# Three chunk copies of an attention kernel moved from ACT to DVE, and its square roots moved up

## The chip, the cores and the metric

The kernel runs on one core of a Trainium2 chip. A core has five engines that run side by side and meet through semaphores: PE (matrix products), DVE (vector work), ACT (activations), POOL (a second, more general vector engine) and SP, which here only issues transfers. The metric is device time in microseconds (us), lower is better.

## The reference

The inputs are x and a context, 16 batches of 64 channels by 512 columns each, in single precision. Per batch:

```python
qp = Wq @ instance_norm(layernorm(x)) + bq;  kp = Wk @ instance_norm(ctx) + bk;  sp = Ws @ ctx + bs
attn = softmax(qp.T @ kp)                      # 512 x 512
mean, mean_sq = attn weighted sums of sp and sp * sp
std = sqrt(relu(mean_sq - mean * mean))
x = x + tanh(g_xattn) * (instance_norm(ctx) * std + mean)
x = x + tanh(g_ffn) * (layernorm(x) @ w.T)     # w dequantised, 512 x 512
```

## The kernel before

Two batches are stacked on the 128 partitions, so there are 8 tiles of 128 x 512 (`t`, or `u` behind attention). Attention works on chunks of 128 columns of one batch: 4 per batch, 8 per tile, 64 in all; `g` is the chunk's number over all tiles, `c` its number in the tile. Every engine has a program of its own in a fixed order written out by hand, and each engine carries out its list strictly in that order; only semaphores tie them together.

One chunk passes through: scores on PE (L292, L293), the row maximum on DVE (L619), the exponential on ACT (L442), the reciprocal of the row sum on DVE (L626), normalising on POOL (L834), the turn on PE (`turn`, four transposes into one of two banks of PSUM, `turn_bank`, L302), the copy of the turned chunk from PSUM to SBUF on ACT (`keep_turned`, L450, into one of three buffers `probs_t`) and the weighted sums on PE (`weigh`, L318). PE turns chunk g, then weighs chunk g-2. A turn needs its bank free, so turn(g) waits for the copy of chunk g-2, and weigh(g) waits for the copy of chunk g.

When a batch's four chunks are weighed, ACT copies the mean (`keep_mean`, L457) and squares it (L460), and DVE subtracts it to the variance (`variance`, L637). Per tile POOL then clips the variance (`relu`, L844), ACT takes its square root (`root`, L465), the normalised context is multiplied with the root, for tile 0 on DVE (`scale_first_context`, L664) and for tiles 1 to 7 on POOL (`scale_context`, L863), and DVE adds the product to X (`after_attention`, L670). The mean was added to X before (`with_mean`, L631).

The last stage, the feed-forward, takes X tile by tile: PE turns it (`turn_x`, L353), ACT copies the turned tile (`keep_xt_hi`, L477), DVE takes the remainder (`keep_xt_lo`, L687), and PE multiplies (L367, L368 with the copy, L374 with the remainder). Beside it DVE takes the row statistics (`row_statistics`, L676, and `finish_row_statistics`, L680 and L682), POOL makes a scale from them (`inverse_deviation2`, L868 and L872), and DVE adds the result to X (`add_ffn`, L695), which SP stores.

The square root needs another function table than the exponential, and is put behind the last exponential for that. In the lists of the engines around the end of attention stand, before the change:

- ACT: exponential of chunk 63, copy of chunk 60, root(0), copies of chunks 61 and 62, keep_mean(7, 0), root(1), copy of chunk 63, keep_xt_hi(0), root(2), root(3), keep_mean(7, 1), keep_xt_hi(1), root(4), keep_xt_hi(2), and so on.
- DVE: reciprocal of chunk 63, with_mean(6), scale_first_context, after_attention(0), variance(7, 0), row_statistics(0), after_attention(1), finish_row_statistics(0), keep_xt_lo(0), row_statistics(1), after_attention(2), finish_row_statistics(1), keep_xt_lo(1), row_statistics(2), variance(7, 1), add_ffn(0), finish_row_statistics(2), after_attention(3), and so on.
- POOL: normalising of chunk 63, the last remainder of the weights (`weights_lo(3)`, L855), scale_context(1), scale_context(2), inverse_deviation2(0), scale_context(3), inverse_deviation2(1), relu(7), scale_context(4), inverse_deviation2(2), scale_context(5), and so on. scale_context(u) waits for root(u), scale_context(1) for scale_first_context too, relu(7) for variance(7, 1).
- PE: turn(62), weigh(60), turn(63), weigh(61), turn_x(0), weigh(62), weigh(63), turn_x(1), the products of tile 0 with the copy, turn_x(2), those with the remainder, and so on.

The functions and the lists that the change touches:

Of the kernel before, what the change touches and what calls it, by code (L numbers as in the profile page):

```python
# [18 lines left out]
def gated_attention_ffn(nc, x, context, params, weight_q_t, scales_zeros, out):  # L19
# [5 lines left out]
    AHEAD_S, AHEAD_E, BEHIND_V = 3, 2, 2  # L25
    SBANKS, PROBS, PROBS_T = 3, 4, 3
    LAST = CHUNKS * TILES
    DMA = 16
    STACK = 6 * DMA
    assert 2 * C == P and N == 512 and GROUPS == 4 and TILES == 8  # L30
# [5 lines left out]
    with ExitStack() as ctx:  # L36
# [9 lines left out]
        def sem(name):  # L46
            return ctx.enter_context(nc.semaphore(name))
# [36 lines left out]
        probs_t = [sb(f"probs_t{i}", [P, N]) for i in range(PROBS_T)]  # L84
# [24 lines left out]
        turn_bank = [bank(f"turn_bank{i}") for i in range(2)]  # L109
# [47 lines left out]
        probs_done = sem("probs_done")  # L157
        turned = sem("turned")
        turned_kept = sem("turned_kept")
        pv_done = sem("pv_done")  # L160
        mean_kept = sem("mean_kept")
        mean_squared = sem("mean_squared")
# [108 lines left out]
        def _(pe):  # L271
# [11 lines left out]
            def scores(g):  # L283
# [5 lines left out]
                if g >= SBANKS:  # L289
# [3 lines left out]
                pe.matmul(score_bank[g % SBANKS][:, :], q_part, k_cross[b][:, :],  # L293
                          start=False, stop=True).then_inc(scores_done, 1)

            def turn(g):

                pe.wait_ge(probs_done, g + 1)
                if g >= 2:
                    pe.wait_ge(turned_kept, g - 1)  # L300
                for i in range(JC):
                    last = pe.transpose(turn_bank[g % 2][:, P * i:P * i + P],  # L302
                                        probs[g % PROBS][:, P * i:P * i + P], ident[:, :])
                last.then_inc(turned, 1)

            def weigh(g):

                t, c = divmod(g, CHUNKS)
                b, j = divmod(c, JC)
                pe.wait_ge(turned_kept, g + 1)  # L310
                if j == 0:
                    pe.wait_ge(s_squared, t + 1)
                    if t > 0:
                        pe.wait_ge(var_done, 2 * (t - 1) + b + 1)
                    elif b == 0:
                        pe.wait_ge(k_lo_done, 1)
                for i in range(JC):
                    last = pe.matmul(pv_bank[b][:, P * j:P * j + P],  # L318
                                     values[t % 2][:, i, b, :, :].rearrange("p a c -> p (a c)"),
                                     probs_t[g % PROBS_T][:, P * i:P * i + P], start=(i == 0), stop=(i == JC - 1))  # L320
                last.then_inc(pv_done, 1)
# [66 lines left out]
            for t in range(TILES):  # L388
                for c in range(CHUNKS):
                    g = CHUNKS * t + c  # L390
# [33 lines left out]
        @block.scalar  # L424
        def _(act):
            def keep_hi(t, which):

                hi, used, done = ((q_hi, q_done, q_hi_done), (k_hi, k_done, k_hi_done))[which]
                act.wait_ge(used, t + 1)
                if t >= 2:  # L430
                    act.wait_ge(stacked[0], STACK * (t - 1))
                    act.wait_ge(stacked[1], STACK * (t - 1))
                act.activation(hi[t % 2][:, :], projection_bank(t, which)[:, :], ACT.Identity,  # L433
                               bias=b_qk[:, which:which + 1]).then_inc(done, 1)

            def exponentials(g):

                c = g % CHUNKS
                act.wait_ge(max_done, g + 1)
                if g >= PROBS:  # L440
                    act.wait_ge(turned, g - PROBS + 1)
                act.activation(probs[g % PROBS][:, :], score_bank[g % SBANKS][:, :], ACT.Exp,  # L442
                               bias=neg_max[:, c:c + 1], accum_out=den[:, c:c + 1]).then_inc(exp_done, 1)

            def keep_turned(g):

                act.wait_ge(turned, g + 1)
                if g >= PROBS_T:
                    act.wait_ge(pv_done, g - PROBS_T + 1)
                act.copy(probs_t[g % PROBS_T][:, :], turn_bank[g % 2][:, :]).then_inc(turned_kept, 1)  # L450

            def keep_mean(t, b):

                act.wait_ge(pv_done, CHUNKS * t + JC * b + JC)
                if t >= 2:
                    act.wait_ge(mean_added, t - 1)
                act.copy(MEAN[t % 2][rows_of(b), :], pv_bank[b][0:C, :]).then_inc(mean_kept, 1)  # L457
                if t >= 1:
                    act.wait_ge(var_done, 2 * (t - 1) + b + 1)
                act.activation(mean_sq[b][C:P, :], pv_bank[b][0:C, :], ACT.Square).then_inc(mean_squared, 1)  # L460

            def root(u):

                act.wait_ge(relu_done, u + 1)
                act.activation(VAR[:, u, :], VAR[:, u, :], ACT.Sqrt).then_inc(root_done, 1)  # L465

            def weights_hi(g):

                act.wait_ge(w_centred, g + 1)
                act.copy(w_hi[:, g, :], w_deq[:, g, :]).then_inc(ffn_hi_done, 1)  # L470

            def keep_xt_hi(u):

                act.wait_ge(xt_turned, u + 1)
                if u >= 2:
                    act.wait_ge(ffn_done, u - 1)
                act.copy(xt_hi[u % 2][:, :], xt_bank[u % 2][:, :]).then_inc(xt_hi_done, 1)  # L477


            act.wait_ge(params_loaded, DMA)  # L480
            act.copy(w_qk_hi[:, :, :], w_qk).then_inc(w_hi_ready, 1)
            act.activation(tanh_g[:, :], gates, ACT.Tanh).then_inc(gates_ready, 1)
            for part, whole, whole_done, part_done in ((x_hi, xn[:, :], xn_done, x_hi_done),
                                                       (c_hi, CTX[:, 0, :], ctxn_done, c_hi_done)):
                act.wait_ge(whole_done, 1)
                act.copy(part[:, :], whole).then_inc(part_done, 1)
            keep_hi(0, 0)
            keep_hi(0, 1)
            act.wait_ge(k_hi_done, 1)
            act.copy(k_same[0][0:C, :], k_hi[0][0:C, :].bitcast(F32)).then_inc(stacked[0], DMA)  # L490
            act.copy(k_cross[0][C:P, :], k_hi[0][0:C, :].bitcast(F32)).then_inc(stacked[0], DMA)
            for g in range(AHEAD_E):
                exponentials(g)

            for t in range(TILES):
                for c in range(CHUNKS):
                    g = CHUNKS * t + c
                    if g + AHEAD_E < LAST:
                        exponentials(g + AHEAD_E)
                    elif c == 6:  # L500
                        root(0)
                    if g > 0:
                        keep_turned(g - 1)
                    if t == 0 and c < 2:
                        keep_hi(1, c)
                    if c == 0 and t > 0 and t + 1 < TILES:
                        keep_hi(t + 1, 1)
                    if c == 2 and t > 0:
                        keep_mean(t - 1, 1)
                    if c == 6 and t + 2 < TILES:  # L510
                        keep_hi(t + 2, 0)
                    if c == 7:
                        keep_mean(t, 0)
                    if t == TILES - 1 and 1 <= c <= 4:
                        weights_hi(c - 1)

            root(1)
            keep_turned(LAST - 1)
            keep_xt_hi(0)
            root(2)  # L520
            root(3)
            keep_mean(TILES - 1, 1)
            keep_xt_hi(1)
            root(4)
            keep_xt_hi(2)
            root(5)
            keep_xt_hi(3)
            root(6)
            keep_xt_hi(4)
            root(7)  # L530
            for u in range(5, TILES):
                keep_xt_hi(u)
# [3 lines left out]
        def _(dve):  # L536
# [85 lines left out]
            def reciprocal(g):  # L622

                c = g % CHUNKS
                dve.wait_ge(exp_done, g + 1)
                dve.reciprocal(rden[:, c:c + 1], den[:, c:c + 1]).then_inc(rden_done, 1)  # L626

            def with_mean(t):

# [4 lines left out]
            def variance(t, b):  # L634

                dve.wait_ge(mean_squared, 2 * t + b + 1)
                dve.tensor_tensor(VAR[rows_of(b), t, :], pv_bank[b][C:P, :], mean_sq[b][C:P, :],  # L637
                                  ALU.subtract).then_inc(var_done, 1)
# [89 lines left out]
            for t in range(TILES):  # L728
                for c in range(CHUNKS):
                    g = CHUNKS * t + c  # L730
# [41 lines left out]
                    if t == TILES - 1:  # L772
                        if c < GROUPS:
                            centre_weights(c)
                        if c == 7:
                            scale_first_context()
                            after_attention(0)

            variance(TILES - 1, 0)
            row_statistics(0)  # L780
            after_attention(1)
# [184 lines left out]
```

## Time and profile before

| | us |
|---|---|
| median of 3 runs | 189.22 |
| the runs | 189.13, 189.22, 190.19 |
| the profiled execution's own time | 190.1 |
| span of its trace | 188.3 |

| engine | busy in the span, us | share |
|---|---|---|
| PE | 169.9 | 90% |
| DVE | 147.1 | 78% |
| ACT | 123.1 | 65% |
| POOL | 118.2 | 63% |

The granted clock of PE is at its full level in all forty slices of the span. All times of rows are us from the start of the span. A row of a timeline has the start, the duration, the engine, the line, the operation, what it writes and reads, and in brackets how long the engine sat idle before it and what ended that. An operation's recorded duration can reach a little over the start of the next one on the same engine.

### The profile page before, as it was taken

The page shows a single profiled execution, that of the slowest core. Times are in us where ns is not written, and L with a number is a line of the kernel's source. Part 1 is how long each engine was busy: PE and PEld are TensorE (multiplying, and loading weights), DVE is VectorE, ACT ScalarE, POOL GpSimd, SP SyncE. Part 2 cuts the span into 40 slices and gives each one's busy share as a digit, 9 for nine tenths or more (in the row PEclk, how much of TensorE's full clock was granted, in tenths as well). Part 3 has the DMA queues.
Part 4 walks back from the last instruction along what each step waited for, and adds up shares of the span by engine and source line. Part 5 has one row for each costly group of instructions (what it writes and reads, how often), then busy time and mean ns, then how long its engine had stood idle before and what let it go on. Part 6 is the DMA issues. An engine that isn't in the chain of part 4 may idle for free.

```text
span 188.3 us, 3539 instructions
## 1 busy us (share of the span) xinstructions
PE 169.9 (90%) x1144; PEld 147.8 (78%) x1144; DVE 147.1 (78%) x316; ACT 123.1 (65%) x268; POOL 118.2 (63%) x142
## 2 busy tenths in 40 slices
PE   0249799999999999999999999999999979789993
PEld 0228599999999989998998999898789778567781
DVE  2888869788978998798889879766248778988851
ACT  2356565996789588669957866995569997223110
POOL 1216667736947795699569669934526969966410
PEclk9999999999999999999999999999999999999999
DMA  5249545761895687289549728353300000111212
GB/s 181 91 121 225 155 111 131 227 148 34 197 308 140 139 286 216 54 205 328 123 108 282 223 59 183 94 118 77 91 0 3 0 0 0 56 57 59 111 56 111
DMA packets 13281, 24.05 MB, mean 128 GB/s; under 512 B 2128, under 2 KB 2256, under 8 KB 13264
## 3 DMA queue, kind: packets, MB, share of 16 engines
q1 hardware_dynamic: 13264, 23.83, 45.8%
q8 instruction: 9, 0.15, 0.3%
q14 instruction: 8, 0.07, 0.1%
HBM read 9.67 MB, written 2.10 MB: 62 GB/s over the span
## 4 chain that ended last, share of the span: by engine, by line
PE 76%; DVE 10%; ACT 5%; issue 3%; DMA 2%; POOL 2%; SPq 0%; ACTq 0%; DVEq 0%
PE pv_bank L318 26%; PE turn_bank L302 13%; PE score_bank L292 8%; PE score_bank L293 8%; PE side_bank L330 3%; PE score_bank L374 3%; PE score_bank L368 2%; PE score_bank L367 2%; PE side_bank L279 2%; DMA params_sb<-in_params 2%; DVE X L670 2%; PE side_bank L281 2%; PE side_bank L280 2%; PE side_bank L339 2%; ACT probs_t L450 1%
## 5 line engine op out<-in xcount | busy, mean ns | idle before, releaser
L834 POOL TENSOR_SCALAR probs<-probs,rden 128x512 f32<-128x512 f32 x64 | 51.3, 803 | 36.1 <-DVE rden L626 35.9
L318 PE MATMUL pv_bank<-probs_t,values 128*128 128x128 f32 x512 | 67.4, 275 | 0.0
L318 PEld LDWEIGHTS pv_bank<-probs_t,values 128*128 128x128 f32 x512 | 63.3, 192 | 2.5 <-issue 1.4
L619 DVE TENSOR_REDUCE neg_max<-score_bank 128x1 f32<-128x512 f32 x64 | 44.0, 687 | 23.6 <-PE score_bank L293 23.2
L442 ACT ACTIVATE probs<-score_bank,neg_max 128x512 f32<-128x512 f32 x64 | 44.0, 688 | 25.0 <-DVE neg_max L619 24.6
L302 PEld LDWEIGHTS turn_bank<-ident,probs 128*128 128x128 f32 x256 | 31.5, 141 | 11.5 <-POOL probs L834 2.4
L302 PE MATMUL turn_bank<-ident,probs 128*128 128x128 f32 x256 | 38.5, 273 | 2.1 <-ACT probs_t L450 1.2
L450 ACT COPY probs_t<-turn_bank 128x512 f32<-128x512 f32 x64 | 37.0, 580 | 0.0
L292 PE MATMUL score_bank<-k_same,q_stack 128*128 128x512 f32 x64 | 31.1, 487 | 2.5 <-DVE k_cross L717 2.5
L293 PE MATMUL score_bank<-k_cross,q_stack 128*128 128x512 f32 x64 | 26.0, 407 | 0.0
L292 PEld LDWEIGHTS score_bank<-k_same,q_stack 128*128 128x128 f32 x64 | 12.7, 198 | 3.5 <-DVE k_cross L717 3.3
L293 PEld LDWEIGHTS score_bank<-k_cross,q_stack 128*128 128x128 f32 x64 | 12.7, 198 | 0.2
L367 PE MATMUL score_bank<-w_hi,xt_hi 128*128 128x512 f32 x32 | 12.8, 401 | 0.0
L368 PE MATMUL score_bank<-w_lo,xt_hi 128*128 128x512 f32 x32 | 12.7, 396 | 0.0
L442 ACT ACTIVATION_READ_ACCUMULATOR probs<-score_bank,neg_max 128x1 f32 x64 | 12.5, 195 | 0.0
L821 POOL TENSOR_TENSOR x_lo<-xn,x_hi 128x512 fp32r<-128x512 f32 x7 | 8.9, 1275 | 5.3 <-DVE x_hi L593 5.3
L279 PE MATMUL side_bank<-x_hi,w_qk_hi 128*128 128x512 f32 x8 | 4.3, 533 | 8.1 <-DVE x_lo L706 8.1
L637 DVE TENSOR_TENSOR VAR<-pv_bank,mean_sq 64x512 f32<-64x512 f32 x16 | 11.1, 694 | 0.5
L626 DVE RECIPROCAL rden<-den 128x1 f32<-128x1 f32 x64 | 9.8, 153 | 1.7 <-ACT probs L442 1.5
L868 POOL TENSOR_TENSOR rstd<-var_eps,power 128x1 f32<-128x1 f32 x8 | 6.7, 834 | 7.0 <-DVE var_eps L682 7.0
L863 POOL TENSOR_TENSOR CTX<-CTX,VAR 128x512 f32<-128x512 f32 x7 | 9.4, 1346 | 2.1 <-ACT VAR L465 2.1
L433 ACT ACTIVATE q_hi<-side_bank,params_sb 128x512 fp32r<-128x512 f32 x8 | 5.5, 687 | 7.5 <-PE side_bank L281 7.5
(101 smaller groups left out, 270.7 us busy)
## 6 DMA issues: line engine op xcount, KB each, us to landing
X<-in_x SPq DMA_DIRECT2D x8, 256.0 KB, 3.1
CTX<-in_context SPq DMA_DIRECT2D x8, 256.0 KB, 3.9
q_stack<-q_hi SPq DMA_DIRECT2D x16, 128.0 KB, 2.3
q_stack<-q_lo SPq DMA_DIRECT2D x16, 128.0 KB, 2.4
ctx_now<-in_context SPq DMA_DIRECT2D x8, 256.0 KB, 3.0
sz<-in_scales_zeros SPq DMA_DIRECT2D x4, 512.0 KB, 6.2
out<-result SPq DMA_DIRECT2D x8, 256.0 KB, 2.0
k_same<-k_hi SPq DMA_DIRECT2D x15, 128.0 KB, 2.4
```

What stands on the lines that cost most here:

```text
L292: pe.matmul(score_bank[g % SBANKS][:, :], q_part, k_same[b][:, :], start=True, stop=False)
L293: pe.matmul(score_bank[g % SBANKS][:, :], q_part, k_cross[b][:, :], start=False, stop=True).then_inc(scores_done, 1)
L302: last = pe.transpose(turn_bank[g % 2][:, P * i:P * i + P], probs[g % PROBS][:, P * i:P * i + P], ident[:, :])
L318: last = pe.matmul(pv_bank[b][:, P * j:P * j + P], values[t % 2][:, i, b, :, :].rearrange("p a c -> p (a c)"), probs_t[g % PROBS_T][:, P * ...
L367: pe.matmul(ffn_bank[u % 2][:, :], hi, w_hi[:, g, :], start=(g == 0), stop=False)
L368: pe.matmul(ffn_bank[u % 2][:, :], hi, w_lo[:, g, :], start=False, stop=False)
L442: act.activation(probs[g % PROBS][:, :], score_bank[g % SBANKS][:, :], ACT.Exp, bias=neg_max[:, c:c + 1], accum_out=den[:, c:c + 1]).then_ ...
L450: act.copy(probs_t[g % PROBS_T][:, :], turn_bank[g % 2][:, :]).then_inc(turned_kept, 1)
L619: dve.tensor_reduce(neg_max[:, c:c + 1], score_bank[g % SBANKS][:, :], AX_X, ALU.max, negate=True).then_inc(max_done, 1)
L626: dve.reciprocal(rden[:, c:c + 1], den[:, c:c + 1]).then_inc(rden_done, 1)
L637: dve.tensor_tensor(VAR[rows_of(b), t, :], pv_bank[b][C:P, :], mean_sq[b][C:P, :], ALU.subtract).then_inc(var_done, 1)
L834: pool.tensor_scalar(probs[g % PROBS][:, :], probs[g % PROBS][:, :], rden[:, c:c + 1], 1.0, ALU.mult, ALU.mult).then_inc(probs_done, 1)
```

## The change

The copies of chunks 61, 62 and 63 are made by DVE (`keep_last_turned`) and counted on a semaphore of their own; PE waits for the one or the other by the chunk's number (`wait_turned_kept`). On ACT they are left out, and root(2) moves ahead of keep_xt_hi(0). ACT's list becomes: copy of chunk 60, root(0), keep_mean(7, 0), root(1), root(2), keep_xt_hi(0), root(3), keep_mean(7, 1), keep_xt_hi(1), and on as before. DVE's becomes: with_mean(6), copies of chunks 61 and 62, scale_first_context, after_attention(0), copy of chunk 63, variance(7, 0), row_statistics(0), after_attention(1), and on as before. POOL's and PE's lists keep their order.

```diff
+    LAST_TURNED = 3
...
+            def wait_turned_kept(g):
+
+                if g < LAST - LAST_TURNED:
+                    pe.wait_ge(turned_kept, g + 1)
+                else:
+                    pe.wait_ge(last_turned_kept, g - (LAST - LAST_TURNED) + 1)
+
             def turn(g):
 
                 pe.wait_ge(probs_done, g + 1)
                 if g >= 2:
-                    pe.wait_ge(turned_kept, g - 1)
+                    wait_turned_kept(g - 2)
...
-                pe.wait_ge(turned_kept, g + 1)
+                wait_turned_kept(g)
...
-                    if g > 0:
+                    if 0 < g <= LAST - LAST_TURNED:
                         keep_turned(g - 1)
...
             root(1)
-            keep_turned(LAST - 1)
+            root(2)
             keep_xt_hi(0)
-            root(2)
             root(3)
...
+            def keep_last_turned(g):
+
+                dve.wait_ge(turned, g + 1)
+                dve.wait_ge(pv_done, g - PROBS_T + 1)
+                dve.tensor_copy(probs_t[g % PROBS_T][:, :], turn_bank[g % 2][:, :]).then_inc(last_turned_kept, 1)
...
-                        if c == 7:
+                        if c == 6:
+                            keep_last_turned(LAST - 3)
+                            keep_last_turned(LAST - 2)
                             scale_first_context()
                             after_attention(0)
 
+            keep_last_turned(LAST - 1)
             variance(TILES - 1, 0)
             row_statistics(0)
             after_attention(1)
```

## Rows read from the trace of the kernel before

**Rows 1.** The chain that ended last: start, us, what; from 140 us on.
```profile
154.62 1.28 POOL CTX L863
...
167.78 0.65 PE side_bank L353 x4
...
185.04 0.75 DVE result L695
```

**Rows 2.** Timeline of ACT from the table of the square root on.
```profile
149.92 1.28 ACT L465 ACT_TABLE_LOAD   x1
151.21 0.63 ACT L465 ACTIVATE VAR<-VAR 128x512 f32<-128x512 f32 x1
151.75 1.05 ACT L450 COPY probs_t<-turn_bank 128x512 f32<-128x512 f32 x2
152.69 0.58 ACT L457 COPY MEAN<-pv_bank 64x512 f32<-64x512 f32 x1
...
153.91 0.63 ACT L465 ACTIVATE VAR<-VAR 128x512 f32<-128x512 f32 x1
```

**Rows 3.** Timeline of PE, the turn of chunk 63.
```profile
152.46 0.63 PE L302 MATMUL turn_bank<-ident,probs 128*128 128x128 f32 x4 [0.90 <-ACT probs_t L450]
```

**Rows 4.** Timeline of DVE.
```profile
149.54 1.41 DVE L631 SCALAR_TENSOR_TENSOR X<-MEAN,tanh_g,X 128x512 f32<-128x512 f32 x1
151.88 1.42 DVE L664 TENSOR_TENSOR CTX<-CTX,VAR 128x512 f32<-128x512 f32 x1 [0.93 <-ACT VAR L465]
153.33 0.75 DVE L670 SCALAR_TENSOR_TENSOR X<-CTX,tanh_g,X 128x512 f32<-128x512 f32 x1
154.11 0.69 DVE L637 TENSOR_TENSOR VAR<-pv_bank,mean_sq 64x512 f32<-64x512 f32 x1
154.83 0.69 DVE L676 BATCH_NORM_STATS2 stats<-X 128x6 f32<-128x512 f32 x1
155.93 0.75 DVE L670 SCALAR_TENSOR_TENSOR X<-CTX,tanh_g,X 128x512 f32<-128x512 f32 x1 [0.40 <-POOL CTX L863]
...
156.81 0.15 DVE L682 TENSOR_SCALAR var_eps<-mean_var 128x1 f32<-128x1 f32 x1
156.99 0.69 DVE L687 TENSOR_TENSOR xt_lo<-side_bank,xt_hi 128x512 fp32r<-128x512 f32 x1
157.60 0.68 DVE L676 BATCH_NORM_STATS2 stats<-X 128x6 f32<-128x512 f32 x1
158.20 0.73 DVE L670 SCALAR_TENSOR_TENSOR X<-CTX,tanh_g,X 128x512 f32<-128x512 f32 x1
...
162.12 1.52 DVE L670 SCALAR_TENSOR_TENSOR X<-CTX,tanh_g,X 128x512 f32<-128x512 f32 x1
...
179.86 0.15 DVE L682 TENSOR_SCALAR var_eps<-mean_var 128x1 f32<-128x1 f32 x1
```

**Rows 5.** Timeline of POOL.
```profile
151.48 1.26 POOL L855 TENSOR_TENSOR w_lo<-w_deq,w_hi 128x512 fp32r<-128x512 f32 x1
...
156.11 1.71 POOL L863 TENSOR_TENSOR CTX<-CTX,VAR 128x512 f32<-128x512 f32 x1 [0.21 <-ACT VAR L465]
...
158.94 1.28 POOL L863 TENSOR_TENSOR CTX<-CTX,VAR 128x512 f32<-128x512 f32 x1
...
161.81 1.28 POOL L863 TENSOR_TENSOR CTX<-CTX,VAR 128x512 f32<-128x512 f32 x1
...
168.21 0.19 POOL L872 TENSOR_TENSOR scale<-rstd,tanh_g 128x1 f32<-128x1 f32 x1
168.35 1.29 POOL L863 TENSOR_TENSOR CTX<-CTX,VAR 128x512 f32<-128x512 f32 x1
...
180.09 0.55 POOL L868 TENSOR_TENSOR rstd<-var_eps,power 128x1 f32<-128x1 f32 x1 [1.53 <-DVE var_eps L682]
```

**Rows 6.** Costliest groups of the page: operation, count, busy, mean ns, idle before.
```profile
L619 DVE TENSOR_REDUCE neg_max<-score_bank 128x1 f32<-128x512 f32 x64 | 44.0, 687 | 23.6 <-PE score_bank L293 23.2
```

**Rows 7.** One line's instructions: DVE's copy L605, ns minimum, median, maximum.
```profile
L605 DVE CAST c_hi<-CTX x7: 585/587/1051, 17.8 to 117.3; 128x512 fp32r<-128x512 f32 x7
```

More of the change, by code:

```diff
@@ L159, in gated_attention_ffn @@
         turned_kept = sem("turned_kept")
+        last_turned_kept = sem("last_turned_kept")
         pv_done = sem("pv_done")
```

## The prediction, made before the change was run

> **What bounds the kernel now.** I read the page's busy shares first, then the chain that ended last, then the timelines of the four engines from 149 us on, where the first changed instruction stands. PE is busy 90% of the span, but that is a mean over stages. From 167.78 us on the chain lies on PE, up to the last result at 185.04 [rows 1]. Before that it does not: it comes from ACT's roots over POOL's multiplication of tile 1's context [rows 1] to DVE, whose list then runs with no gap to speak of until PE takes over. So the change is worth what it does to the moment at which DVE gets through its list between 150 and 168 us. Work taken from ACT or PE in that stretch counts only if DVE gets something earlier from it.
>
> Two stalls of DVE are plain idle time there: 0.93 us for root(0) ahead of L664, and 0.40 for POOL ahead of after_attention(1) [rows 4]. A third kind is hidden in durations. L664 took 1.42 us beside a POOL operation that ended at 151.48 + 1.26 = 152.74, and itself ended at 153.30; after_attention(3) took 1.52 beside one that ended at 161.81 + 1.28 = 163.09, and ended at 163.64 [rows 4, 5]. The same operation takes 0.75 without company. So a DVE operation with two operands in SBUF that meets a running POOL operation ends 0.55 us behind POOL's end, and it works the other way too: scale_context(2) took 1.71 in place of 1.28 beside after_attention(1), ending 1.71 - 1.28 = 0.43 late, as if begun at 156.54, 0.14 before DVE's end at 156.68 [rows 4, 5]. Whichever starts first keeps the other out. An operation with one operand in SBUF is not held: L676 at 154.83 takes its 0.69 beside scale_context(1), which runs from 154.62 to 155.90 [rows 1, 4].
>
> **The change part by part.** *PE.* turn(63) sat idle 0.90 us for ACT's copy of chunk 61, which stood behind the table load and root(0) [rows 2, 3]. That copy now starts on DVE behind with_mean(6), at 149.54 + 1.41 = 150.95 [rows 4], in place of 151.75. So turn(63) and weigh(61) come some 0.8 us earlier. Nothing follows from it: PE's next instruction is turn_x(0), which waits for after_attention(0), and weigh(62) and weigh(63) stand behind that in PE's list. This gain is worth 0.
>
> *The copies' price.* No DVE copy from PSUM is in the trace. The nearest rows are the maximum, which reads the same shape from PSUM in 0.69 [rows 6], and the copy from SBUF, 0.59 alone and 1.05 when held [rows 7]. I take 0.69, with 0.59 and 1.05 as ends. Their own gain of 0.1 each is too small to matter below; being held would matter and is a rival.
>
> The Trainium skill speaks of this in "VectorE: DVE Perf Modes", section "Why PSUM operands drop a tier": a PSUM operand rules out the mode that uses both SBUF ports, so by that page the copy from PSUM would neither run at the doubled rate nor be held by POOL. By that rule the sum is the one below and the third rival falls; by the row of the SBUF copy alone the rival stands. No run here shows the copy itself.
>
> *Copies 61 and 62.* 150.95 + 2 x 0.69 = 152.33. Then comes L664, which root(0) releases at 151.84 as before; it meets the POOL operation that runs until 152.74 and ends at 153.30 as before. The two copies are hidden by the 0.93 idle and 0.45 of the hold; without that cover they would cost 1.38. after_attention(0) is unchanged, 153.33 to 154.08.
>
> *The roots.* root(0) stays at 151.21. Without the two copies the mean's copy starts at 151.75 in place of 152.69, so root(1), 153.91 - 152.69 = 1.22 behind it, starts at 152.97 and ends at 153.61, 0.94 earlier [rows 2]; root(2) follows at once and ends by 153.61 + 0.63 = 154.24. scale_context(1), released by root(1) at about 153.68, finds after_attention(0) running since 153.33 and begins in effect at 154.08 - 0.14 = 153.94; it ends at 153.94 + 1.28 = 155.22, not 154.62 + 1.28 = 155.90. scale_context(2) has its root by then and follows with no gap, 155.2 to 156.48. Before, it came only at 156.11, behind after_attention(1), for want of root(2) [rows 5].
>
> *Copy 63.* It stands on DVE between after_attention(0) and variance(7, 0): 154.08 + 0.69 = 154.77, variance from 154.80, statistics 0.72 later (154.83 - 154.11) at 155.52, after_attention(1) due 0.6 to 0.7 behind, 156.0 to 156.2. This one is not hidden: the 0.40 idle covers part, and after_attention(1) is due 0.1 to 0.3 later than its 155.93 of before.
>
> *What is late next.* At 156.1 POOL is inside scale_context(2). So after_attention(1) is held and ends at 156.48 + 0.55 = 157.03, where it was 155.93 + 0.75 = 156.68: +0.35. This hardly depends on the copy's price, since POOL's end sets it. Then DVE's list runs on as before, 0.35 later: L682 at 156.81 + 0.35 = 157.16, after_attention(2) due at 158.55. POOL is idle now, where before it was still late from its own hold. It takes L868 0.23 behind L682 (180.09 - 179.86), which lasts 0.55, L872 0.08 behind that (the step from L682's end at 180.01 to L868), and scale_context(3) 0.14 behind L872's start [rows 4, 5]: 157.16 + 0.23 + 0.55 + 0.08 + 0.14 = 158.16, until 159.44. Before, scale_context(3) started at 158.94, behind after_attention(2); now it starts 0.39 ahead of it. after_attention(2) is held and ends at 159.44 + 0.55 = 159.99, where it was 158.20 + 0.73 = 158.93: +1.06.
>
> From there POOL's relu(7) waits for DVE's variance(7, 1), so scale_context(4) and the hold of after_attention(3) come again at the same distance. The +1.06 passes on whole to PE at 167.78, which had waited for DVE, and to the end. ACT's and PE's waits in that stretch all hang on DVE's after_attention or on PE's products, which have over half a microsecond to spare.
>
> The sum: PE 0, copies 61 and 62 0, copy 63 and the first collision +0.35, the second +0.71; together +1.06. Against the profiled execution that is 190.1 + 1.06 = 191.16 (span 188.3 to 189.36). The runs' median, 189.22, lies 0.9 below that execution, so the forecast for a median is 189.22 + 1.06 = 190.28, say 190.3.
>
> **The rivals.** *Only the first collision.* If DVE reaches after_attention(2) before POOL starts scale_context(3), the price stays at +0.35: 189.6. The margin is 0.39, and some 0.3 if L687 follows L682 sooner than the 0.18 of before. For it: the margin is a difference of two sums of several steps each, POOL's taken from other tiles. Against: all steps but the first are DVE's and POOL's own work with nothing to wait for.
>
> *DVE goes first (not slower).* If after_attention(1) starts ahead of scale_context(2), both collisions fall, POOL is again the one held, and DVE's list runs as before. The point of decision is whether scale_context(2) starts before 156.0 to 156.2. Priced at 0.59 a copy from 153.99 on, as the pipeline allows where nothing is held, after_attention(1) is due at 155.9 and the 0.40 idle is just used up: 0.0 to -0.2, 189.0 to 189.2. For it: so it was before [rows 4, 5]. Against: scale_context(2) would have to come 0.8 later than its root allows.
>
> *The copies are held too (slower by over 1%).* If a copy from PSUM needs the port like L605's slow case, copy 62 waits for POOL until 152.74 and ends near 153.3, so L664 ends at 154.0 and after_attention(0) at 154.8, +0.7; copy 63 is then held by scale_context(1), 1.3 more, and the second collision stays at +0.7: +2.7 in all, 191.9. The point of decision is the duration of copy 62: 0.69 or over 1. Against: none of the PSUM readers is stretched.
>
> *It doesn't do what it says.* If something else held root(1), say keep_mean's wait for weigh(59), POOL would start no earlier and only copy 63's 0.1 to 0.3 would be left: 189.4. But weigh(59) stands two places ahead of turn(63) in PE's list, with weigh(60) between them, and PE had been idle since 151.56 when turn(63) began [rows 3], so weigh(59) was done well before 151.56.
>
> **How the numbers follow.** The forecast 0.62; only the first collision 0.14; DVE first 0.09; copies held 0.07; no earlier root 0.04; something that the rows don't show 0.04, half to each side. What a measurement can tell from no change is about 1%, 1.9 us: below 187.3 or above 191.1. The forecast and all rivals but the held copies lie inside. Slower by over 1%: 0.07 and some of the unknown, 0.10. Faster: all idle time of DVE in the stretch together is 1.33 us, less than 1.9, so 0.03. Within: 0.87. The range goes from 189.0 (DVE first) to 191.1 (the forecast with another half hold of 0.8); it leaves out the held copies, half of the unknown cases and the lower part of "DVE first".
>
> **What would show it right or wrong.** In the changed profile: copies on DVE of about 0.69 at 150.9, 151.6 and 154.0; turn(63) near 151.6; L664 again ending at 153.3; root(1) at 153.0; scale_context(1) stretched beyond 1.28 and scale_context(2) right behind it; after_attention(1) and after_attention(2) both stretched to over 0.9 us, where they were 0.75 and 0.73; turn_x(4) on PE 1.06 later, and the same distance to the end. I am wrong if the two after_attention rows stay at 0.75 (the collisions don't come), if copy 62 is over 1 us, or if turn_x(4) comes before 167.78.

## The result, and the profile after

The changed kernel takes 190.32 us (median of 12 runs, 189.62 to 191.25), the kernel before 189.34 beside it (12 runs, 188.94 to 190.19). The ratio is 1.0054, 95% interval 1.0030 to 1.0078: 0.6 to 1.5 us slower, some 1.0. The profiled execution took 191.25 with a span of 189.5, against 190.1 and 188.3.

Up to the last exponential the two programs are the same, and there the changed one is 0.09 us late (its start is at 148.71, before at 148.62). What follows is best read from that point on. The row of the kernel before from which its times are counted:

```profile
148.62 0.71 ACT L442 ACTIVATE probs<-score_bank,neg_max 128x512 f32<-128x512 f32 x1
```

ACT's timeline of the changed kernel, which answers to [rows 2]:

```profile
148.71 0.71 ACT L451 ACTIVATE probs<-score_bank,neg_max 128x512 f32<-128x512 f32 x1
...
150.00 1.28 ACT L474 ACT_TABLE_LOAD   x1
151.29 0.63 ACT L474 ACTIVATE VAR<-VAR 128x512 f32<-128x512 f32 x1
151.83 0.56 ACT L466 COPY MEAN<-pv_bank 64x512 f32<-64x512 f32 x1
...
153.03 1.15 ACT L474 ACTIVATE VAR<-VAR 128x512 f32<-128x512 f32 x2
```

root(1) starts at 153.03 where it was 153.91, and root(2) is in the same row, right behind it. That part of the change does what it says. PE's turn of chunk 63, which answers to [rows 3], has lost its wait:

```profile
151.79 0.63 PE L311 MATMUL turn_bank<-ident,probs 128*128 128x128 f32 x4
...
154.23 0.66 PE L362 MATMUL side_bank<-ident,X 128*128 128x128 f32 x4 [0.92 <-DVE X L684]
```

It starts at 151.79, not 152.46, and has no idle in front of it. The next row shows what that is worth: turn_x(0) starts at 154.23, 0.09 later than the 154.14 of before, after 0.92 us of waiting for DVE, where it was 0.15. The stall has only moved. DVE's timeline, which answers to [rows 4]:

```profile
149.62 1.43 DVE L645 SCALAR_TENSOR_TENSOR X<-MEAN,tanh_g,X 128x512 f32<-128x512 f32 x1
150.97 1.27 DVE L640 COPY probs_t<-turn_bank 128x512 f32<-128x512 f32 x2
152.17 1.22 DVE L678 TENSOR_TENSOR CTX<-CTX,VAR 128x512 f32<-128x512 f32 x1
153.43 0.75 DVE L684 SCALAR_TENSOR_TENSOR X<-CTX,tanh_g,X 128x512 f32<-128x512 f32 x1
154.09 0.68 DVE L640 COPY probs_t<-turn_bank 128x512 f32<-128x512 f32 x1
154.81 0.69 DVE L651 TENSOR_TENSOR VAR<-pv_bank,mean_sq 64x512 f32<-64x512 f32 x1
155.53 0.69 DVE L690 BATCH_NORM_STATS2 stats<-X 128x6 f32<-128x512 f32 x1
156.14 0.95 DVE L684 SCALAR_TENSOR_TENSOR X<-CTX,tanh_g,X 128x512 f32<-128x512 f32 x1
...
158.62 1.47 DVE L684 SCALAR_TENSOR_TENSOR X<-CTX,tanh_g,X 128x512 f32<-128x512 f32 x1
...
163.28 1.52 DVE L684 SCALAR_TENSOR_TENSOR X<-CTX,tanh_g,X 128x512 f32<-128x512 f32 x1
```

Look at the L684 rows, the additions after attention: 0.75 for tile 0, then 0.95 and 1.47 for tiles 1 and 2, which were 0.75 and 0.73, and 1.52 for tile 3 as before. POOL's timeline, which answers to [rows 5], shows with whom they meet:

```profile
151.57 1.27 POOL L872 TENSOR_TENSOR w_lo<-w_deq,w_hi 128x512 fp32r<-128x512 f32 x1
153.74 2.81 POOL L880 TENSOR_TENSOR CTX<-CTX,VAR 128x512 f32<-128x512 f32 x2 [0.89 <-ACT VAR L474]
157.45 0.56 POOL L885 TENSOR_TENSOR rstd<-var_eps,power 128x1 f32<-128x1 f32 x1 [0.91 <-DVE var_eps L696]
158.09 0.19 POOL L889 TENSOR_TENSOR scale<-rstd,tanh_g 128x1 f32<-128x1 f32 x1
158.24 1.30 POOL L880 TENSOR_TENSOR CTX<-CTX,VAR 128x512 f32<-128x512 f32 x1
...
164.21 1.00 POOL L885 TENSOR_TENSOR rstd<-var_eps,power 128x1 f32<-128x1 f32 x1
```

scale_context(1) and (2) are now one block, until 153.74 + 2.81 = 156.55, and after_attention(1), due at 156.14, ends at 157.09, 0.54 behind the block. scale_context(3) starts at 158.24, 0.38 ahead of after_attention(2), and ends at 159.54; after_attention(2) ends at 160.09, 0.55 behind it. Before it ended at 158.93, so it is 1.16 late, 1.07 without the 0.09 that came from ahead of the change. turn_x(4), with which the chain goes over to PE, starts at 168.94 where it was 167.78 [rows 1]: again 1.16. Its row, and that of the last result:

```profile
168.94 0.66 PE L362 MATMUL side_bank<-ident,X 128*128 128x128 f32 x4 [0.62 <-DVE X L684]
```
```profile
186.21 0.75 DVE L709 SCALAR_TENSOR_TENSOR result<-score_bank,scale,X 128x512 f32<-128x512 f32 x1 [2.06 <-PE score_bank L383]
```

The start of the last result lies 37.50 us behind the start of the last exponential; before it was 36.42. The difference, 1.08, is the whole loss.

### The profile page after: what moved, and what is told of

The parts are those of the page before. It is cut to its first block, busy times and chain, and to the rows that moved or that the text cites. A ratio compares the mean times of both kernels' runs of the same rounds, so it can differ in the third digit from the quotient of the medians.

```text
span 189.5 us, 3539 instructions
## 1 busy us (share of the span) xinstructions
PE 170.4 (90%) x1144; PEld 148.0 (78%) x1144; DVE 149.5 (79%) x319; ACT 121.3 (64%) x265; POOL 117.2 (62%) x142
## 4 chain that ended last, share of the span: by engine, by line
PE 74%; DVE 13%; issue 4%; ACT 3%; DMA 2%; POOL 2%; SPq 0%; ACTq 0%; DVEq 0%
PE pv_bank L327 25%; PE turn_bank L311 13%; PE score_bank L295 7%; PE score_bank L294 7%; PE side_bank L339 3%; PE score_bank L383 3%; PE side_bank L281 3%; PE score_bank L377 2%; PE score_bank L376 2%; DVE X L684 2%; DMA params_sb<-in_params 2%; PE side_bank L283 2%; PE side_bank L282 2%; PE side_bank L348 2%; DVE stats L690 1%
## 5 line engine op out<-in xcount | busy, mean ns | idle before, releaser
L311 PEld LDWEIGHTS turn_bank<-ident,probs 128*128 128x128 f32 x256 | 32.1, 143 | 10.5 <-issue 1.4
L311 PE MATMUL turn_bank<-ident,probs 128*128 128x128 f32 x256 | 39.1, 276 | 0.9 <-POOL probs L851 0.5
L459 ACT COPY probs_t<-turn_bank 128x512 f32<-128x512 f32 x61 | 35.3, 579 | 0.0
L885 POOL TENSOR_TENSOR rstd<-var_eps,power 128x1 f32<-128x1 f32 x8 | 6.7, 835 | 8.8 <-DVE var_eps L696 8.8
L856 POOL TENSOR_TENSOR values<-values 128x512 f32<-128x512 f32 x8 | 9.1, 1139 | 2.8 <-DVE values L660 2.8
L442 ACT ACTIVATE q_hi<-side_bank,params_sb 128x512 fp32r<-128x512 f32 x8 | 5.5, 687 | 7.5 <-PE side_bank L283 7.4
```

Source lines behind the costliest of these rows:

```text
L311: last = pe.transpose(turn_bank[g % 2][:, P * i:P * i + P], probs[g % PROBS][:, P * i:P * i + P], ident[:, :])
```

## The experiments

All the versions below share the program up to the last exponential, but their executions reach it between 147.4 and 149.5 us. So beside each measured ratio stands the distance in its profile from the start of the last exponential (L442 in the kernel before) to the start of the last result (L695), which that scatter does not touch. For the kernel before it is 36.42. Each distance comes from one profile, but the parts of it that no version changes repeat closely: from the last exponential to turn_x(0) it is 5.52 or 5.53 in all eleven profiles, and from turn_x(7) to the last result 6.25 or 6.26. PE's granted clock is at its full level (2.4 GHz) from the last exponential to the end in all of them.

The kernel before ran again beside the versions of each round: its median was 189.84 beside e1 to e4, 189.77 beside e5 to e7 and 189.92 beside e8 and e9. The ratios go by these runs, not by the 189.34 above, and they are not the quotients of the medians (for e1 that would be 189.46 / 189.84 = 0.998).

| version | ratio to before, 95% interval | distance, us | against before |
|---|---|---|---|
| changed kernel | 1.0054 (1.0030 to 1.0078) | 37.50 | +1.08 |
| e1, POOL waits twice | 0.9994 (0.9971 to 1.0018) | 36.52 | +0.10 |
| e3, POOL waits once | 1.0005 (0.9974 to 1.0035) | 36.77 | +0.35 |
| e2, copy 63 on ACT | 1.0051 (1.0024 to 1.0078) | 37.48 | +1.06 |
| e4, before with root(2) up | 1.0089 (1.0057 to 1.0121) | 38.15 | +1.73 |
| e5, copy 63 on ACT and both waits | 0.9960 (0.9930 to 0.9991) | 35.94 | -0.48 |
| e6, before with two meetings less | 0.9966 (0.9935 to 0.9998) | 36.00 | -0.42 |
| e7, e5 and e6 together | 0.9932 (0.9908 to 0.9957) | 35.15 | -1.27 |
| e8, e7 with the mean later | 0.9895 (0.9860 to 0.9929) | 34.48 | -1.94 |
| e9, e6 with the mean later | 0.9918 (0.9883 to 0.9953) | 35.34 | -1.08 |

Two explanations of the loss were to be told apart: that POOL's multiplications, coming earlier, keep DVE's additions out (called the port theory below), or that DVE simply has three copies more to do (work). The profile alone can't decide this, since both make DVE late.

**Take the meetings away, keep the work (e1).** POOL waits for DVE's addition before its next multiplication:

```diff
             def scale_context(u):
 
                 pool.wait_ge(root_done, u + 1)
                 if u == 1:
                     pool.wait_ge(scaled_done, 1)
+                if u in (2, 3):
+                    pool.wait_ge(x2_done, u)
```

> The changed kernel, with POOL's scale_context(2) and scale_context(3) waiting until DVE has done after_attention(1) and after_attention(2). Port theory: both after_attention rows are back at 0.75 us, only the place of copy 63 in DVE's list is left of the price: +0.2 us against the kernel before (189.3 to 189.7). Rival, that DVE's three added copies (about 1.9 us of work) are the price and the stretched rows only show them: the waits can only delay POOL, so the time stays at the changed kernel's 190.3 or is longer.

Measured: 189.46 us (median of 12), ratio 0.9994 against the kernel before, no difference to be seen, and 0.10 us more by the profile. The same three copies are on DVE, and adding two waits to POOL took the loss away. DVE's and POOL's timelines show the rows back at their price:

```profile
156.31 0.73 DVE L684 SCALAR_TENSOR_TENSOR X<-CTX,tanh_g,X 128x512 f32<-128x512 f32 x1
...
158.56 0.73 DVE L684 SCALAR_TENSOR_TENSOR X<-CTX,tanh_g,X 128x512 f32<-128x512 f32 x1
```
```profile
157.19 1.29 POOL L882 TENSOR_TENSOR CTX<-CTX,VAR 128x512 f32<-128x512 f32 x1 [1.71 <-DVE X L684]
...
159.44 1.29 POOL L882 TENSOR_TENSOR CTX<-CTX,VAR 128x512 f32<-128x512 f32 x1
```

POOL now sits idle for 1.71 us ahead of scale_context(2), and the kernel is 0.98 us faster by the profile than the changed one for it.

**Take only the second away (e3).** The same edit with `if u in (3,)`.

> The changed kernel, with scale_context(3) alone waiting for after_attention(2). Port theory: after_attention(1) stays stretched at 0.95, after_attention(2) is back at 0.75; +0.35 us against the kernel before (189.5 to 189.9), so 0.7 less than the changed kernel. Rival (work): as the changed kernel, 190.3.

Measured: 189.73 us, ratio 1.0005; by the profile +0.35. DVE's two rows are as expected, the first held and the second not:

```profile
155.88 0.95 DVE L684 SCALAR_TENSOR_TENSOR X<-CTX,tanh_g,X 128x512 f32<-128x512 f32 x1
...
158.35 0.74 DVE L684 SCALAR_TENSOR_TENSOR X<-CTX,tanh_g,X 128x512 f32<-128x512 f32 x1
```

So the first meeting with copy 63 in DVE's list is worth 0.35, and the second the other 0.73.

**Take work away, keep the meetings (e2).** Copy 63 goes back to ACT, behind the two early roots:

```diff
             root(1)
             root(2)
+            keep_turned(LAST - 1)
             keep_xt_hi(0)
...
-            keep_last_turned(LAST - 1)
             variance(TILES - 1, 0)
```

PE's `wait_turned_kept` is told accordingly that chunk 63 counts on ACT's semaphore again.

> The changed kernel with the copy of chunk 63 back on ACT, behind root(2); copies 61 and 62 stay on DVE, the roots stay early. Port theory: DVE reaches after_attention(1) 0.7 us earlier but finds scale_context(2) at work since 155.2 and ends when it did: the row is stretched to 1.4 or more, the rest as in the changed kernel, +1.0 us against the kernel before (190.1 to 190.6). Rival (work): DVE has 0.7 us less to do, so +0.35 (189.7).

Measured: 190.80 us, ratio 1.0051, and by the profile +1.06, as if nothing had been taken from DVE. The row of after_attention(1) has taken up what the copy left:

```profile
155.38 1.55 DVE L686 SCALAR_TENSOR_TENSOR X<-CTX,tanh_g,X 128x512 f32<-128x512 f32 x1
...
158.45 1.47 DVE L686 SCALAR_TENSOR_TENSOR X<-CTX,tanh_g,X 128x512 f32<-128x512 f32 x1
```
```profile
153.58 2.80 POOL L881 TENSOR_TENSOR CTX<-CTX,VAR 128x512 f32<-128x512 f32 x2 [0.91 <-ACT VAR L475]
```

It starts earlier and ends at 156.93, 0.55 behind POOL's block of two, 153.58 + 2.80 = 156.38. The work theory wanted 0.7 us less and falls here.

**Make the meetings without any copy (e4).** In the kernel before, root(2) moves up by two places on ACT, and nothing else:

```diff
             root(1)
+            root(2)
             keep_turned(LAST - 1)
             keep_xt_hi(0)
-            root(2)
             root(3)
```

> The kernel before with root(2) moved up behind root(1), ahead of the copy of chunk 63 and keep_xt_hi(0); no copy on DVE. Port theory: scale_context(2) now follows scale_context(1) with no gap, at 155.86, a hair ahead of after_attention(1), which ends at 157.69 (+1.0); scale_context(3) then starts at 158.8, ahead of after_attention(2) due at 159.2, which ends at 160.65: +1.7 us against the kernel before (190.7 to 191.3), with no work added anywhere. If DVE wins the near tie at 155.9: 0. Rival (work): no change, 189.3.

Measured: 191.10 us, ratio 1.0089, by the profile +1.73: 1.6 times the loss of the whole change, from one instruction that became ready earlier. DVE's rows, and POOL's block of scale_context(1) and (2):

```profile
154.83 1.75 DVE L670 SCALAR_TENSOR_TENSOR X<-CTX,tanh_g,X 128x512 f32<-128x512 f32 x1 [0.39 <-POOL CTX L863]
...
158.10 1.47 DVE L670 SCALAR_TENSOR_TENSOR X<-CTX,tanh_g,X 128x512 f32<-128x512 f32 x1
```
```profile
153.53 2.50 POOL L863 TENSOR_TENSOR CTX<-CTX,VAR 128x512 f32<-128x512 f32 x2 [1.87 <-ACT VAR L465]
```

The 0.39 of waiting for scale_context(1) is still there, and behind it the same operation that took 0.75 takes 1.75, because scale_context(2) started at the moment at which scale_context(1) let DVE go. The near tie at 155.9 went to POOL.

**Keep what is good in the change (e5).** e2 with the two waits of e1.

> Copies 61 and 62 on DVE, copy 63 on ACT, early roots, and scale_context(2) and (3) waiting for after_attention(1) and (2). Port theory: after_attention(1) starts as soon as scale_context(1) lets it, some 0.4 us earlier than in the kernel before, both rows at 0.75: -0.4 us against the kernel before (ratio 0.998), 1.4 less than without the waits. Rival (work): the waits change nothing, as in the run without them (ratio 1.005).

Measured: 189.05 us against 189.77, ratio 0.9960; by the profile -0.48. The first addition that gains is after_attention(1):

```profile
155.04 0.73 DVE L686 SCALAR_TENSOR_TENSOR X<-CTX,tanh_g,X 128x512 f32<-128x512 f32 x1
```

It starts 6.83 us behind the last exponential (at 148.21 in this profile), where it was 7.31: this is the 0.48. scale_context(1), for which it had waited, ends at 6.60 instead of 7.27, since root(1) comes earlier with copies 61 and 62 gone from ACT. So the change holds a gain, once POOL doesn't get in front of DVE with it. Whether root(2)'s move adds to it behind the two waits was not tried.

**Take away meetings that were there before (e6).** In the kernel before:

```diff
             scale_context(3)
+            scale_context(4)
             inverse_deviation2(1)
             relu(TILES - 1)
-            scale_context(4)
...
             row_statistics(3)
-            with_mean(TILES - 1)
             add_ffn(1)
...
                 if u + 1 < TILES:
                     row_statistics(u + 1)
+                if u == 4:
+                    with_mean(TILES - 1)
                 add_ffn(u - 1)
```

> The kernel before with two later collisions taken out and no copy moved: POOL's scale_context(4) ahead of inverse_deviation2(1) and relu(7), so that it is done when DVE reaches after_attention(3), and DVE's with_mean(7) moved behind row_statistics(5), where PE is the bound. Port theory: after_attention(3) falls from 1.52 to 0.75 us and the 1.34 of with_mean(7) leaves DVE's full stretch; PE's idle 1.18 and 0.62 us ahead of turn_x(3) and turn_x(4) shrink to some 0.4: -1.0 to -1.5 us (ratio 0.992 to 0.995). If DVE were not the bound there: no change.

Measured: ratio 0.9966, by the profile -0.42. The size was missed by more than half. turn_x(4) did come 1.12 earlier from the last exponential (18.04 us behind it, not 19.16), and after_attention(3) takes 0.75. But with_mean(7) met scale_context(7) at its new place, and PE paid for it:

```profile
169.91 1.35 DVE L631 SCALAR_TENSOR_TENSOR X<-MEAN,tanh_g,X 128x512 f32<-128x512 f32 x1
```
```profile
169.42 1.30 POOL L864 TENSOR_TENSOR CTX<-CTX,VAR 128x512 f32<-128x512 f32 x1
```
```profile
172.93 0.66 PE L353 MATMUL side_bank<-ident,X 128*128 128x128 f32 x4 [0.62 <-DVE X L670]
```

The rows are DVE's with_mean(7), POOL's scale_context(7) and PE's turn_x(6). I had priced the move at 0.75 and not asked who runs beside the new place.

**Both together (e7).**

> The two before together: copies 61 and 62 on DVE, copy 63 on ACT, early roots, the two waits on POOL, scale_context(4) earlier and with_mean(7) later. Port theory: the gains add until PE has no idle left in the stretch, 1.18 + 0.62 us: -1.4 to -1.8 us against the kernel before (ratio 0.990 to 0.993), faster than both kernels.

Measured: 188.41 us against 189.77, ratio 0.9932; by the profile -1.27, short of the -1.4 to -1.8 by the same meeting, which is there too (with_mean(7) takes 1.35, and PE sits idle 0.63 us ahead of turn_x(6)). It is still more than e5 and e6 give one by one, 0.48 + 0.42 = 0.90: in e6 DVE sits idle 0.28 us ahead of after_attention(4), for which the profile names no releaser, and in e7 it doesn't. Why was not tried.

**The mean one tile later (e8 and e9)**, `if u == 5`, where POOL has no context left. e8 is e7 with this, e9 is e6 with it:

> The version with all edits, with_mean(7) one tile later, behind row_statistics(6). In the version before, it stood beside scale_context(7), took 1.35 us and made PE idle 0.63 ahead of turn_x(6). One tile later POOL has no context left to multiply and turn_x(7) comes only behind the products with the remainder. Port theory: with_mean(7) at 0.75, no idle of PE ahead of turn_x(6) and turn_x(7): 0.6 us less than before, ratio 0.989 to 0.992. If the order alone counts and not the meeting: as before, 0.993.

> The kernel before with scale_context(4) earlier and with_mean(7) behind row_statistics(6), no copy moved, no root moved. Port theory: as the version with it one tile earlier but 0.6 us less: ratio 0.992 to 0.995; it stays some 0.4 us behind the version with all edits, by the earlier after_attention(1).

Measured: 188.05 us against 189.92, ratio 0.9895 for e8 (6 runs), and 0.9918 (188.27, 7 runs) for e9, at the lower edge of its 0.992 to 0.995. In e8's profile with_mean(7) is unheld and turn_x(6) has no idle:

```profile
173.91 0.73 DVE L647 SCALAR_TENSOR_TENSOR X<-MEAN,tanh_g,X 128x512 f32<-128x512 f32 x1
```
```profile
172.85 0.66 PE L363 MATMUL side_bank<-ident,X 128*128 128x128 f32 x4
```

By the profiles the step from u = 4 to u = 5 is worth 0.67 (35.15 to 34.48) and 0.66 (36.00 to 35.34). e8 is 0.86 ahead of e9 by the profiles, more than the 0.4 expected; the medians' ratios, 0.9895 and 0.9918, put it at 0.44 with intervals that overlap, so how much the copies and the early roots bring on top of the rest is not settled. e8 is the fastest of all versions, by some 2.0 us ahead of the kernel before and, by way of it, 3.0 ahead of the changed one, beside which it did not run (1.0054 - 0.9895 = 0.016 of 189).

## Why the prediction was right

Forecast 190.3, measured 190.32. A median that close has luck in it, since the runs scatter by over 1 us; the steps are what can be judged, and they can be judged one by one. The profiles put the loss at 1.08 where 1.06 was forecast; the medians of 12 runs each differ by 190.32 - 189.34 = 0.98. The prediction took about 1% for what a measurement can tell; with these runs the interval of the ratio reaches 0.24% to either side, enough to tell 0.54% from nothing.

- *PE's earlier turn is worth 0.* Right: turn(63) came 0.67 earlier (0.76 without the 0.09 from ahead of the change) and turn_x(0) 0.09 later, with 0.92 of idle ahead of it in place of 0.15.
- *The copies at 0.69, unheld.* Right: 0.68, and 1.27 for two, while POOL was at work beside both. The rival of held copies falls. The rule of the Trainium skill that the prediction set beside it ("VectorE: DVE Perf Modes", "Why PSUM operands drop a tier") agrees with the trace: the copies took 0.68, neither the 0.43 of the cast from SBUF that ran with POOL idle (L593, below) nor a stretched time.
- *Copies 61 and 62 hidden.* Right: L678 ended at 153.39, before at 153.30, and the 0.09 was there already at the last exponential. Its duration fell from 1.42 to 1.22, because it started later, behind the copies, and POOL's operation ended as before.
- *root(1) at 152.97, scale_context(1) held by after_attention(0), scale_context(2) with no gap, ending at 156.48.* Right: 153.03, and 156.55 for the block; without the 0.09, 152.94 and 156.46. e4, with root(1) where it was and no copy on DVE, shows separately that root(2) alone can bring the meetings about.
- *First meeting +0.35, whatever the copy costs.* Right: 157.09 - 156.68 - 0.09 = 0.32 in the changed kernel, 0.35 in e3. That POOL's end sets it, and not the copy, is e2's finding.
- *Second meeting, decided by a margin of 0.39.* Right: 0.38. The rival with only the first meeting fell with it, as e3 gives its time, +0.35.
- *The rest passes on whole.* Right: +1.07 at after_attention(2), 1.07 at turn_x(4), 1.08 at the last result.
- *DVE goes first* was the way to end level; e1 forces that order and ends level, +0.10.

Three smaller readings in the prediction don't hold, and the sum uses none of them. *An operation with one operand in SBUF is not held* is too wide, and L605's 0.59 is not its price alone. These are rows of the kernel before, of DVE and of POOL:

```profile
13.96 0.43 DVE L593 CAST x_hi<-xn 128x512 fp32r<-128x512 f32 x1
...
50.08 0.58 DVE L605 CAST c_hi<-CTX 128x512 fp32r<-128x512 f32 x1
```
```profile
49.18 1.21 POOL L839 TENSOR_TENSOR values<-values 128x512 f32<-128x512 f32 x1
```

L605 at 50.08 ends at 50.66, 0.27 behind POOL's 50.39, and all seven of L605, those of 0.59 and that of 1.05 alike, end 0.27 to 0.29 behind the end of a POOL operation. That is how a held row ends, so by these rows this cast, with one operand in SBUF, is held each time. The similar L593 at 13.96, with POOL idle, took 0.43. Among the rows used, only the statistics and, now, the copy from PSUM run unheld beside POOL. So the lower price of 0.59 in *DVE goes first* had no unheld row behind it, and the third rival took its hold from an operation of another kind. *Two places ahead of turn(63)* is three for weigh(59), with turn(62) and weigh(60) between, which leaves the argument as it is. And *half a hold of 0.8* at the top of the range is a whole one by [rows 4], 1.52 - 0.75 = 0.77.

What I did not see is that a part of the change was worth keeping: e5 shows 0.48 us of gain from the two hidden copies and the root(1) that they let forward. I had put PE's and ACT's gains at 0 for this kernel, which was right for it, and had not asked what order on POOL would have let them through.

## What to carry to other kernels

An operation that becomes ready earlier can cost time, without any work added, when it shares something exclusive with the engine that bounds the stage: before you free an engine, list which pairs will newly meet and who starts first. A held operation doesn't show as idle time; it shows as a longer row, so compare durations of the same line with each other and not only the waits. And where a slack engine gets in front of the bound one, a wait that looks like a loss (1.71 us of idle on POOL in e1) can be the repair.

## What the runs showed of the hardware

The price of a meeting was very even: an addition after attention, a DVE operation with two SBUF operands, that found a multiplication on POOL at work ended 0.54 to 0.55 us behind POOL's recorded end, in the changed kernel twice, in e2 and in e4, against a duration of 0.75 alone. The Trainium skill says in "SBUF — State Buffer", section "Who interferes with whom", that a DVE instruction with two SBUF inputs contends with a POOL instruction that reads SBUF, that the pair of ports which they share is an exclusive lock, and that the order of issue decides who is blocked; the trace agrees, with these numbers. The runs show that the two keep each other out and who goes first; that it is a port where they meet, no run shows by itself.

I had not expected how small the held operation may be. POOL's L885 on a single column per partition, 0.56 us alone, takes 1.00 beside after_attention(3) in the changed kernel (164.21 to 165.21, DVE's addition ending at 163.28 + 1.52 = 164.80): it takes 0.44 longer and ends 0.41 behind DVE, although it moves almost nothing. The kernel before has the same at 163.05, so it is no part of the loss.

And the instructions before the last exponential, the same in all versions, took from 147.4 to 149.5 us over eleven profiles, a spread twice as large as the effect studied here. Where it arises was not tried; it is why the distance from a common point told the versions apart at 0.1 us when the medians could not.
